# The three bf16 parts of a group's softmax shift made on Pool before the turn, instead of on VectorE after it

## The reference

```python
scores = jnp.einsum('bqhd,bkhd->bhqk', q, k) * SCALE
bias = slopes[:, None, None] * rel[None, :, :]
scores = jnp.where(causal[None, None], scores + bias[None], -jnp.inf)
attn = jax.nn.softmax(scores, axis=-1)
out = jnp.einsum('bhqk,bkhd->bqhd', attn, v).reshape(B, S, HIDDEN)
return out @ w_proj + b_proj
```

## Time and profile before

| what | value |
|---|---|
| time, median of 3 runs | 909.03 us (908.92 to 909.49) |
| the profiled execution | 909.71 us, of which the span from first to last instruction is 907.5 us |
| PE busy | 852.9 us (94%) |
| DVE busy | 750.5 us (83%) |
| ACT busy | 473.3 us (52%) |
| POOL busy | 301.1 us (33%) |
| mean granted TensorE clock | 0.976 of full speed |

### The profile page before, as it was taken

One profiled execution on the slowest core, in us unless ns is written; L12 is line 12 of the kernel. 1 busy time (PEld: TensorE's weight loads), 2 busy tenths in 40 slices (PEclk: granted clock), 3 DMA queues, 4 the chain that ended last, 5 costly groups with the idle time before them and its releaser, 6 DMA issues.

```text
span 907.5 us, 12065 instructions
## 1 busy us (share of the span) xinstructions
PE 852.9 (94%) x4031; PEld 400.7 (44%) x4031; DVE 750.5 (83%) x1613; ACT 473.3 (52%) x904; POOL 301.1 (33%) x310
## 2 busy tenths in 40 slices
PE   5999878899989999899999999999999999999996
PEld 3435424454447454344444444443444444444442
DVE  5699999999998875888999999995247799767877
ACT  4777654666652032112888888888734555343100
POOL 1057999899984000050121111211110443000000
PEclk8888999999999999999999999999999999999999
DMA  9300060300005015510322202200052000000011
GB/s 345 110 0 1 1 278 0 139 1 1 1 0 206 2 48 182 177 41 6 86 80 81 58 26 79 81 2 3 1 177 73 1 0 1 0 0 1 12 40 41
DMA packets 22135, 54.06 MB, mean 60 GB/s; under 512 B 6085, under 2 KB 12869, under 8 KB 19066
## 3 DMA queue, kind: packets, MB, share of 16 engines
q1 hardware_dynamic: 22074, 53.30, 17.2%
HBM read 44.70 MB, written 8.39 MB: 59 GB/s over the span
## 4 chain that ended last, share of the span: by engine, by line
PE 58%; DVE 8%; SPq 2%; issue 1%; POOL 1%; ACT 1%; DMA 1%; POOLq 0%; DVEq 0%
PE ps L1222 17%; PE ps L1084 7%; PE ps L1233 6%; PE ps L1064 5%; PE ps L1048 3%; PE ps L1051 3%; PE ps L1143 3%; PE ps L1123 3%; PE ps L993 3%; PE ps L1106 2%; SPq L320 2%; DVE ps L1489 1%; DVE mrow L1496 1%; PE ps L802 1%; DVE mrow L1493 1%
## 5 line engine op out<-in xcount | busy, mean ns | idle before, releaser
L481 POOL TENSOR_TENSOR hC<-hs,C_sb 128x512 f32<-128x512 f32 x128 | 160.3, 1270 | 50.9 <-ACT C_sb L685 31.5
L755 ACT ACTIVATE prob<-ps 128x512 f32<-128x512 f32 x288 | 158.9, 602 | 28.3 <-PE ps L1067 12.6
L973 PE MATMUL ps<-hC,identf 128*128 128x512 f32 x256 | 139.1, 646 | 13.4 <-POOL hC L481 12.1
L614 ACT ACTIVATE ps<-dtT,nA 128x512 f32<-128x512 f32 x128 | 88.2, 690 | 50.4 <-DVE hs L1377 47.2
L504 POOL TENSOR_SCALAR_AFFINE_SELECT prob<-prob 128x256 f32<-128x256 f32 x96 | 39.0, 406 | 224.1 <-ACT prob L755 224.1
L1064 PE MATMUL ps<-stack 123*128 123x512 bf16 (+3 forms) x384 | 108.4, 327 | 1.3 <-ACT prob L755 1.1
L1496 DVE TENSOR_REDUCE mrow<-ps 128x1 f32<-128x512 f32 x128 | 81.9, 683 | 7.3 <-PE ps L1051 5.3
L1084 PE MATMUL ps<-prob,V 128*32 128x512 f32 (+3 forms) x768 | 81.6, 498 | 0.7 <-POOL prob L504 0.7
L973 PEld LDWEIGHTS ps<-hC,identf 128*128 128x128 f32 x256 | 47.6, 201 | 72.9 <-POOL hC L481 56.1
L1222 PE MATMUL ps<-hT,wg 128*128 128x512 f32 (+1 forms) x176 | 79.1, 592 | 0.0
L1222 PE MATMUL ps<-hT,wu 128*128 128x512 f32 (+1 forms) x176 | 79.1, 592 | 0.0
(11 more groups left out here) (201 smaller groups left out, 1320.1 us busy)
## 6 DMA issues: line engine op xcount, KB each, us to landing
stack<-parts_dram SPq DMA_DIRECT2D x96, 128.0 KB
wmod<-in_wmod SPq DMA_DIRECT2D x4, 1536.0 KB, 12.5
parts_dram<-qkp SPq DMA_DIRECT2D x16, 384.0 KB, 2.6
wmod<-in_wmod SPq DMA_DIRECT2D x4, 1024.0 KB, 10.5
wattn<-in_wattn SPq DMA_DIRECT2D x1, 3072.0 KB, 10.3
wg<-in_wg SPq DMA_DIRECT2D x1, 2752.0 KB, 11.1
wu<-in_wu SPq DMA_DIRECT2D x1, 2752.0 KB, 10.7
wd<-in_wd SPq DMA_DIRECT2D x1, 2560.0 KB, 10.6
```

The source lines that it names most:

```text
L481: pool.tensor_tensor(hC[:, c, :], hs[:, c, :], C_sb[:, m % 2, :], ALU.mult).then_inc(S["hc_done"], 1)
L614: A_(ps[:, DA_BANK + c % 2, :], dtT[:, c, half(h)], ACT.Exp, scale=nA[:, c * NS + s:c * NS + s + 1]).then_inc(S["da_done"], 1)
L755: A_(prob[:, u % 4, j, :], ps[:, 3 + F % 3, :], ACT.Exp, scale=-1.0).then_inc(S["exp_done"], 1)
L973: mm(ps[:, c, :], identf[:], hC[:, c, :], start=False, stop=(s == NS - 1), skip_group_check=True).then_inc(S["sum_done"], 1)
```

## The change

`split_shift`'s arithmetic moves ahead of the turn. A new function on POOL, `shift_parts(g)`, waits for `r_rdy`, and makes the three bf16 parts of `rr` in its own layout, 128 partitions by 3 x 32, in `rp`, with `rd` as the fp32 remainder: four instructions, each waiting for the one before. It stands in POOL's order ahead of the masks of step 32 of a group (for group 0 ahead of all masks). PE's turn is now a plain bf16 product of `rp` (96 columns, as the weights) with a bf16 identity, instead of an fp32 transpose of `rr`, and waits for `rp_done` instead of `r_rdy`. DVE copies the 96 x 128 result to `r3` in one instruction. `load_shift` reads `r3` in its new layout, with as many bytes.

```diff
-        rd = at("rd", 31, [GH * NT, P], off=128)
-        r3 = at("r3", G_AT + 53, [GH * NT, 3, P], BF16)
+        rp = at("rp", 31, [P, 3, GH * NT], BF16, off=128)
+        rd = at("rd", 31, [P, GH * NT], off=384)
+        r3 = at("r3", G_AT + 53, [3 * GH * NT, P], BF16)
...
-                         .rearrange("o h (i c) -> o (h i) c", c=P), r3[:, r, :], rrow[g % 3])
+                         .rearrange("o h (i c) -> o (h i) c", c=P), r3[GH * NT * r:GH * NT * (r + 1), :], rrow[g % 3])
...
+            def shift_parts(g):
+                pool.wait_ge(S["r_rdy"], g + 1)
+                if g:
+                    pool.wait_ge(S["rt_mm"], g)
+                pool.tensor_copy(rp[:, 0, :], rr[:]).then_inc(S["rp_link"], 1)
+                pool.wait_ge(S["rp_link"], 3 * g + 1)
+                pool.tensor_tensor(rd[:], rr[:], rp[:, 0, :], ALU.subtract).then_inc(S["rp_link"], 1)
+                pool.wait_ge(S["rp_link"], 3 * g + 2)
+                pool.tensor_copy(rp[:, 1, :], rd[:]).then_inc(S["rp_link"], 1)
+                pool.wait_ge(S["rp_link"], 3 * g + 3)
+                pool.tensor_tensor(rp[:, 2, :], rd[:], rp[:, 1, :], ALU.subtract).then_inc(S["rp_done"], 1)
+
+            shift_parts(0)
             for F in range(NG * FU):
                 U, j = F // GH, F % GH
                 on = PAIRS[U % NU]
+                if F % FU == FU - GH and F // FU + 1 < NG:
+                    shift_parts(F // FU + 1)
...
                 ring_free(T_POS[g])
-                pe.wait_ge(S["r_rdy"], g + 1)
-                pe.transpose(ps[0:GH * NT, T_POS[g] % 3, 0:P], rr[:], identf[:]).then_inc(S["rt_mm"], 1)
+                pe.wait_ge(S["rp_done"], g + 1)
+                mm(ps[0:3 * GH * NT, T_POS[g] % 3, 0:P], rp[:].rearrange("p r n -> p (r n)"), identb[:], start=True, stop=True) \
+                    .then_inc(S["rt_mm"], 1)
...
-                pr = ps[0:GH * NT, T_POS[g] % 3, 0:P]
-                v.tensor_copy(r3[:, 0, :], pr).then_inc(S["r_part"], 1)
-                v.wait_ge(S["r_part"], g * 3 + 1)
-                tt(rd[:], pr, r3[:, 0, :], ALU.subtract).then_inc(S["r_part"], 1)
-                v.wait_ge(S["r_part"], g * 3 + 2)
-                v.tensor_copy(r3[:, 1, :], rd[:]).then_inc(S["r_part"], 1)
-                v.wait_ge(S["r_part"], g * 3 + 3)
-                tt(r3[:, 2, :], rd[:], r3[:, 1, :], ALU.subtract).then_inc(S["rt_evac"], 1)
+                v.tensor_copy(r3[:], ps[0:3 * GH * NT, T_POS[g] % 3, 0:P]).then_inc(S["rt_evac"], 1)
```

More of the change, by code:

```diff
@@ L239, in program @@
                   "qk_mm qk_evac qk_split v_mm v_done "
-                  "s_mm m_done r_part rec_done r_rdy rt_mm rt_evac st_mm exp_done pv_done ot_evac ot_tr ao_done v_ones "
-                  "neg_mm neg_done bounded masked aot_tr aot_evac pj_mm pj_y x2 x2pre bias1 "
+                  "s_mm m_done  rec_done r_rdy rt_mm rt_evac st_mm exp_done pv_done ot_evac ot_tr ao_done v_ones "
+                  "neg_mm neg_done rp_link rp_done bounded masked aot_tr aot_evac pj_mm pj_y x2 x2pre bias1 "
                   "g_mm f_exp f_sgn f_y0 f_out dn_mm dn_y0 dn_sgn dn_y dn_done out_dma dchain pchain achain").split():
```

## The result

The median fell from 909.03 us to 903.27 us, 7 runs each. The ratio is 0.9941, with a 95% interval of 0.9929 to 0.9952, so the change gains 5.4 us (4.4 to 6.5). The profiled execution took 903.27 us with a span of 901.5 us.

What follows compares the result with a forecast made beforehand. PE and DVE were both nearly full, with DVE bounding 6.9 us of a group's 29.2 and PE the other 22.3. Six turns x 0.54 us gave -3.3 us, other terms nothing: median 909.03 to 905.7 us, range 904.0 to 908.4.

Steps and rivals of the forecast that it cites:

- That PE gets time back at six turns, from DVE: At the turns of groups 1 to 6, PE waits less for DVE: six turns x 0.54 us = 3.3 us.
- DVE gets back 0.8 us: At each turn, one copy of 0.28 us on DVE replaces the split's four instructions of 1.07 us.
- Both gaps close: 0.54 us. The rest of DVE's 0.8 us becomes idle time, because PE is late next: PE's waits at the two score units behind a turn, 0.45 us for the split and 0.09 us for the next reduction, vanish.
- more than the gaps: Rival: PE runs freer behind the turn, weights loaded earlier; up to 4.8 + 0.5 = 5.3 us gained, 903.7 us; chance 0.09.
- The first and the last turn, nothing: At the first turn PE is the later engine, before the last DVE is idle; neither gains anything.
- POOL costs nothing: POOL's four new instructions per turn take 1.0 to 1.9 us, ending 0.9 us or more before PE's turn.
- PE's turn, nothing to either side: The bf16 product replacing the fp32 transpose gains or loses up to 0.06 us a turn; counted as nothing, 0.5 us either side.
- No contention of POOL and DVE: DVE's custom instructions and reductions of units 0 to 3 do not slow beside POOL's work; custom instructions stay at 0.33 us.
- The range: Forecast time from 904.0 us, taking in most of the freer PE, to 908.4 us, taking in half the gain.

## Why the prediction was right and wrong

- **That PE gets time back at six turns, from DVE:** right. Leaving out the DVE instructions alone gives all but 0.03 us a turn, putting them back takes it all away.
- **DVE gets back 0.8 us:** right. The copy takes 0.277 us. From the copy's start to the next one are 0.20 instead of 1.07 us, so start to start it is 0.87.
- **"Both gaps close: 0.54 us. The rest of DVE's 0.8 us becomes idle time, because PE is late next":** the step that failed. PE's time does come from DVE, but the term was 0.82 us for a group, not 0.54 (0.87 at unit 11). The first half measured as forecast, 0.58 us up to unit 7 with 0.03 from the shorter turn. The second was an assumption: I followed PE for two units behind the turn and took it to be the later engine from there on, since the chain showed only PE. DVE still had its whole lag there, with the normalisation and three reductions of 0.6 us each in front of it, while PE asks for a new bank every 0.45 us. Another 0.28 us waited at units 9 and 10. The case called "more than the gaps", with 0.8 us a turn and a chance of 0.09, came nearest, by luck: not for its reason (weights loaded earlier) but by DVE's lag.
- **The view that would have pointed there:** the waits of the weight loads in the kernel before. I had used only the one row of PE's matmuls. Another row of the same answer counts three units a turn that waited for a plain reduction on DVE:

```profile
PEld ps L1048 <- DVE mrow L1493: 4.6, 18, 0.3
```

  They are units 7, 9 and 10. In the changed kernel no weight load of L1065 (the same line) waits for L1510 (the same reduction) any more. The row says where to look, not what it costs: the same view of the changed kernel has 13 weight loads of L1065 that wait 9.6 us for L1513, with no wait of a product for it. The price comes from the distances from start to start.
- **The first and the last turn, nothing:** right. The first group takes 29.6 us before and after, and behind the last `rr` there are 285.5 and 285.4 us.
- **POOL costs nothing:** right. Four instructions of 0.21 to 0.25 us, 1.2 us from `rr` to the last end, within the 1.0 to 1.9 us taken; 1.6 us to spare.
- **PE's turn, nothing to either side:** right within the 0.06 us allowed, 0.09 us to the next start instead of 0.12.
- **No contention of POOL and DVE:** right. The custom instructions take 0.328 us in the median against 0.330 before, and the stretch is no longer with POOL's work than without it. The sentence in the Trainium skill's "Perfetto Trace Analysis", section "Optimizing Scalar/DVE Operations", that moving work between these two might not help does not bear on these instructions; the narrower rule in its "SBUF — State Buffer", section "Who interferes with whom", agrees with the runs.
- **The range** ended at 904.0, only 0.2 us past the cap of DVE's whole time that its own working named (4.8 us from 909.0, 904.2), so it left next to nothing for the scatter of the medians: the two medians of 7 runs differ by 5.8 us, of which the stretch of the change shows 5.0.

## What to carry to other kernels

When two engines pass work through a small ring, take an instruction's time on the late one as a lag, and follow it unit by unit until the late engine has caught up; the first wait shows where the lag is paid first, not how much it costs. Cap the gain by the whole time removed, and let the range reach past that cap by the scatter of the runs. To test such a reading, put the removed work back in steps: the line of cost against added time shows slope and free part at once.

## What was not expected of the hardware

The chain and the matmul waits showed no gap at units 9 and 10, though they started 0.12 and 0.16 us late in the kernel before (0.58 and 0.60 us after their predecessors, against 0.46 and 0.44 after the change). A product of 512 bf16 columns is listed with 0.38 us, while the next one can start after 0.22 us; a wait shorter than the difference hides inside the modelled end of the one before. Among the products only the distance from start to start shows it; the weight loads are marked with a wait.
